# Rotary embedding from pairs of projected tiles, and layer 1's stack rows in another order

## What is computed

```python
# layer 1, on q and on k: head of 8 dimensions, halves t1 (0..3) and t2 (4..7)
t1, t2 = (t[..., :half], t[..., half:])
return jnp.concatenate([t1 * cos - t2 * sin, t1 * sin + t2 * cos], axis=-1)
...
# layer 2, on the 32 rotated dimensions of q: neighbours x0, x1
xr = xh.reshape(xh.shape[:-1] + (d // 2, 2))
x0, x1 = (xr[..., 0], xr[..., 1])
rot = jnp.stack([x0 * cos - x1 * sin, x0 * sin + x1 * cos], axis=-1)
...
x = x + _layernorm(_attn1(_layernorm(x)))      # layer 1
x = x + _layernorm(_layer2(_layernorm(x)))     # layer 2: attention, then the experts
```

## Time and profile before

| | |
|---|---|
| runs of the kernel before, us | 1727.74, 655.25, 657.92 (median 657.92) |
| the profiled execution, us | 656.71 |
| span of its trace, us | 655.0 |
| mean clock granted to PE | 0.947 of full |
| busy: PE, DVE, ACT, POOL, us | 564.1, 401.0, 310.4, 212.5 |
| DMA packets, data | 26657, 46.55 MB |

### The profile page before, as it was taken

The page is one execution under the profiler, slowest core; times in us unless marked ns, Lnnn a source line. Parts: engine busy times, 40 slices in busy tenths (PEclk is TensorE's granted clock), DMA queues, the critical chain, the costliest instruction groups (busy, mean ns, idle before and its releaser), DMA issues.

```text
span 655.0 us, 10075 instructions
## 1 busy us (share of the span) xinstructions
PE 564.1 (86%) x3634; PEld 311.1 (48%) x3634; DVE 401.0 (61%) x932; ACT 310.4 (47%) x589; POOL 212.5 (32%) x276
## 2 busy tenths in 40 slices
PE   3884998888887898999978999999999998899873
PEld 1732444444343454544435555545576446644642
DVE  6374877685684565675765675756646765534453
ACT  2311765666453664466434655554445432563221
POOL 4562444153442632660353211414322110220101
PEclk9685999999888899999998999999999999999987
DMA  9322113111334433211571122225314120000000
GB/s 269 103 88 102 39 46 111 59 53 41 122 111 77 114 88 128 110 67 61 103 182 46 56 51 42 47 77 116 92 21 86 30 51 1 19 2 1 0 18 16
DMA packets 26657, 46.55 MB, mean 71 GB/s; under 512 B 3216, under 2 KB 12336, under 8 KB 26032
## 3 DMA queue, kind: packets, MB, share of 16 engines
q1 hardware_dynamic: 26608, 45.91, 25.8%
HBM read 27.62 MB, written 17.83 MB: 69 GB/s over the span
## 4 chain that ended last, share of the span: by engine, by line
PE 60%; DVE 15%; SPq 6%; DMA 5%; ACT 5%; issue 4%; POOL 3%; DVEq 0%; POOLq 0%; ACTq 0%
PE ps L564 13%; PE ps L627 11%; PE ps L521 9%; PE ps L492 6%; DVE NM L1123 4%; PE ps L515 4%; PE ps L494 3%; PE ps L489 3%; PE ps L748 2%; DVE stats L1107 2%; PE ps L677 2%; SPq L441 2%; PE ps L571 2%; DMA KS<-scr_k 2%; PE ps L610 1%
## 5 line engine op out<-in xcount | busy, mean ns | idle before, releaser
L1123 DVE TENSOR_REDUCE NM<-ps 128x1 f32<-128x512 f32 (+3 forms) x352 | 219.3, 638 | 119.2 <-PE ps L494 111.5
L785 ACT ACTIVATE PG<-ps 128x512 f32<-128x512 f32 x320 | 181.5, 596 | 169.3 <-PE ps L521 86.8
L521 PE MATMUL ps<-QS,K 128*128 128x512 f32 x320 | 117.9, 453 | 0.0
L494 PE MATMUL ps<-maskb,identb 128*128 128x128 bf16 x512 | 108.8, 231 | 0.0
L564 PE MATMUL ps<-PG,V 128*32 128x512 f32 (+3 forms) x1024 | 97.9, 456 | 8.8 <-POOL PG L1070 6.2
L492 PE MATMUL ps<-K,QS 96*128 96x256 f32 (+3 forms) x256 | 83.6, 371 | 10.4 <-DVE NM L1123 10.2
L489 PE MATMUL ps<-KS,QS 96*128 96x256 bf16 (+3 forms) x256 | 72.3, 317 | 16.7 <-DVE NM L1123 15.6
L515 PE MATMUL ps<-QS,KS 128*128 128x128 bf16 (+3 forms) x256 | 64.1, 313 | 12.2 <-DMA QS<-MP 6.7
L1029 POOL TENSOR_TENSOR whole<-terms 128x512 f32<-128x512 f32 x28 | 35.5, 1269 | 109.4 <-DVEq L1216 107.8
L521 PEld LDWEIGHTS ps<-QS,K 128*128 128x128 f32 x320 | 50.9, 191 | 39.1 <-issue 19.6
L494 PEld LDWEIGHTS ps<-maskb,identb 128*128 128x128 bf16 x512 | 51.4, 100 | 38.0 <-issue 30.5
(11 more groups left out here) (153 smaller groups left out, 670.5 us busy)
## 6 DMA issues: line engine op xcount, KB each, us to landing
scr<-QC SPq DMA_DIRECT2D x24, 512.0 KB, 3.1
QS<-scr SPq DMA_DIRECT2D x32, 256.0 KB
QS<-scr_q SPq DMA_DIRECT2D x16, 288.0 KB
KS<-scr_k SPq DMA_DIRECT2D x16, 288.0 KB
QS<-scr SPq DMA_DIRECT2D x64, 64.0 KB
...
```

The lines of the kernel that those rows point to most:

```text
L494: return pe.matmul(dst[:, P * (k - 1):P * k], identb[:], maskb[:, 0, :], start=False, stop=True)
L521: mm = pe.matmul(bank.rearrange("p (h q) -> p h q", h=HG), keys[:, SEQ[n] % 2, P * j:P * j + P], QS2[:, heads, P * i:P * i + P], start=(ke ...
L785: act.activation(PG[:, n % 2, unit_place(LAYER[n], (u + k) % UNITS), :], ps[:, ST0 + (u + k) % 3, :], ACT.Exp, scale=scale).then_inc(exp_d ...
L1123: dve.tensor_reduce(dst, src, AX.X, ALU.max, negate=True).then_inc(fill_read, 1)
```

## The change

Three things are changed together.

1. **No turned projections.** In layer 1, `q1` projects two tiles whose rows are mixed: tile u holds the first halves of q (rows 0 to 63) and the second halves of k (rows 64 to 127), tile u + 1 the second halves of q and the first halves of k. `k1` has no projection any more. The new `rotation_of_pair` on DVE makes of the two tiles first u x cos and (u + 1) x sin, which POOL adds, then (u + 1) x cos and u x sin, which POOL subtracts. In layer 2, `ropeA` with part 0 (or 2) projects the even dimensions of two head groups into one tile and the odd ones into the next, by a view of the weights that takes every second column; parts 1 and 3 have no projection. Both tiles stay in their banks until the second job has read them.
2. **Slots.** `k1` goes into the slot of `q1`; `ropeA` 1 goes into the slot of `ropeA` 0, and `ropeA` 3 into that of `ropeA` 2. `ropeB` stays where it was.
3. **DRAM side.** Half tiles of 64 rows are stored (`store1`: 16 DMAs of 64 KB instead of 8 of 128 KB), layer 2's rotated rows are loaded by two DMAs of 16 rows for each part instead of one of 32 (`load2`: 8 DMAs for a head group instead of 6), and it waits for both tiles of the pair. In `load1` the 72 stack rows are ordered with the 24 (part, dimension) rows outside and the three copies inside; before, the three copies were outside. The weights are loaded without the turned halves, for layer 1 in four DMAs instead of one, three of them with runs of 64 numbers.

```diff
-        names = ("ln1", "ln1n", "x1T", "q1", "k1", "parts1", "parts1b", "store1")
-        return [(*slot, name, b, 0) for slot, name in zip((*at, at[-1]), names)]
+        return [(*slot, name, b, 0) for slot, name in zip((*at[:4], at[3], *at[5:], at[-1]), names)]
...
-                ((12, 3), "qabs", 1), ((12, 3), "kst2", 0), ((13, 0), "ropeA", 0), ((13, 1), "ropeB", 0),
-                ((13, 1), "ropeA", 1), ((13, 2), "ropeB", 1), ((13, 2), "ropeA", 2), ((13, 3), "ropeB", 2),
-                ((13, 3), "ropeA", 3), ((14, 0), "ropeB", 3), ((16, 3), "load2", 0), ((17, 0), "load2", 1),
+                ((12, 3), "qabs", 1), ((12, 3), "kst2", 0), ((13, 0), "ropeA", 0), ((13, 0), "ropeA", 1), ((13, 1), "ropeB", 0), ((13, 2), "ropeB", 1),
+                ((13, 2), "ropeA", 2), ((13, 2), "ropeA", 3), ((13, 3), "ropeB", 2), ((14, 0), "ropeB", 3), ((16, 3), "load2", 0), ((17, 0), "load2", 1),
...
-        QKV_LOADS = ((wqkv_sb[:], wqkv[:]), (rope1_sb[:], rope1[:]))
+        QKV_LOADS = ((wqkv_sb[:, 0:2, 0:64], wqkv[:, 0].rearrange("c (a m) -> c a m", a=2)),
+                     (wqkv_sb[:, 0, 64:P], wqkv[:, 2, 64:P]), (wqkv_sb[:, 1, 64:P], wqkv[:, 2, 0:64]),
+                     (wqkv_sb[:, 2], wqkv[:, 4]), (rope1_sb[:], rope1[:]))
...
-                    sp.dma_start(scr_q[b, a], qp[:, a, :]).then_inc(stored1, 16)
-                    sp.dma_start(scr_k[b, a], kp[:, a, :]).then_inc(stored1, 16)
-                    if a < 2:
-                        sp.dma_start(scr_k[b, 3 + a], kp[:, a, :]).then_inc(stored1, 16)
+                    sp.dma_start(scr_q[b, a, 0:64], up[0:64, a, :]).then_inc(stored1, 16)
+                    sp.dma_start(scr_q[b, a, 64:P], vp[0:64, a, :]).then_inc(stored1, 16)
+                    for copy in ((a, 3 + a) if a < 2 else (a,)):
+                        sp.dma_start(scr_k[b, copy, 0:64], vp[64:P, a, :]).then_inc(stored1, 16)
+                        sp.dma_start(scr_k[b, copy, 64:P], up[64:P, a, :]).then_inc(stored1, 16)
...
-                sp.dma_start(QS1[0:72, heads, :], bass.AP(q_parts.tensor, q_parts.offset, [[0, 3], *q_parts.ap]))\
-                  .then_inc(stack1_in[g], 16)
-                sp.dma_start(KS1[0:72, heads, :], bass.AP(k_parts.tensor, k_parts.offset, [[P * T, 3], *k_parts.ap]))\
-                  .then_inc(stack1_in[g], 16)
+                rows = [[H * T, 24], [0, 3], [1, HG * T]]
+                sp.dma_start(QS1[0:72, heads, :], bass.AP(scr_q, (3 * b * P + HG * g) * T, rows)).then_inc(stack1_in[g], 16)
+                rows = [[H * T, 24], [P * T, 3], [1, HG * T]]
+                sp.dma_start(KS1[0:72, heads, :], bass.AP(scr_k, (5 * b * P + HG * g) * T, rows)).then_inc(stack1_in[g], 16)
...
-                    sp.dma_start(QS2[DK2 * a + LAT:DK2 * a + DK2, heads, :].bitcast(F32),
-                                 scr_2[b, 2 + g, a].rearrange("(h d) t -> d h t", h=HG)).then_inc(stack2_in[g], 16)
+                    for odd in range(2):
+                        rows = scr_2[b, 2 + pair + odd, a, 64 * (g % 2):64 * (g % 2) + 64]
+                        sp.dma_start(QS2[DK2 * a + LAT + odd:DK2 * a + DK2:2, heads, :].bitcast(F32),
+                                     rows.rearrange("(h i) t -> i h t", h=HG)).then_inc(stack2_in[g], 16)
...
             def ropeA(b, part):
+                if part % 2:
+                    return
                 pe.wait_ge(xT2_ready, b + 1)
+                w = wqr_sb[:, part:part + 2, :].rearrange("c g (h i two) -> c (g h) i two", i=ROPE // 2, two=2)
                 for k in range(2):
-                    project(BANK0["ropeA", b, part] + k, wqr_sb[:, k, part, :], xT2[:])
+                    project(BANK0["ropeA", b, part] + k, w[:, :, :, k], xT2[:])
...
+            def rotation_of_pair(u, j, second, table):
+
+                if j >= 2:
+                    dve.wait_ge(job_done[j % 2], j // 2)
+                for k in range(2):
+                    bank = u + (1 - k if second else k)
+                    last = dve.tensor_tensor(terms[:, j % 2, k, :], full(bank), table[:, k, :], ALU.mult)
+                    if second:
+                        last.then_inc(bank_read[bank_of(bank)], 1)
+                if second:
+                    dve.wait_ge(*was_read(u))
+                    dve.sem_inc(terms_ready, 1)
+                else:
+                    last.then_inc(terms_ready, 1)
```

More of the change, by code:

```diff
@@ L108, in beside @@
                 ((7, 1), "x2T", 0), ((7, 2), "kst", 0), ((7, 2), "latv", 0), ((7, 3), "qabs", 0), ((7, 3), "kst2", 0),
-                ((8, 0), "qabs", 1), ((8, 0), "ropeA", 0), ((8, 1), "ropeB", 0), ((8, 1), "ropeA", 1),
-                ((8, 2), "ropeB", 1), ((8, 2), "ropeA", 2), ((8, 3), "ropeB", 2), ((8, 3), "ropeA", 3),
-                ((9, 0), "ropeB", 3), ((9, 1), "load2", 0), ((9, 3), "load2", 1), ((10, 2), "load2", 2),
+                ((8, 0), "qabs", 1), ((8, 0), "ropeA", 0), ((8, 0), "ropeA", 1), ((8, 1), "ropeB", 0), ((8, 2), "ropeB", 1),
+                ((8, 2), "ropeA", 2), ((8, 2), "ropeA", 3), ((8, 3), "ropeB", 2), ((9, 0), "ropeB", 3), ((9, 1), "load2", 0), ((9, 3), "load2", 1), ((10, 2), "load2", 2),
                 ((11, 2), "load2", 3))
@@ L168 @@
         TURN_OF.append(_n[0])
-    _n = [a + t for a, t in zip(_n, TAKES.get(_stage, (0, 0, 0, 0)))]
+    _takes = "ropeA2" if _stage == "ropeA" and _part % 2 else _stage
+    _n = [a + t for a, t in zip(_n, TAKES.get(_takes, (0, 0, 0, 0)))]
 BANK = []
@@ L453, in load2 @@
             def load2(b, g):
-                tiles = [QTILE["qabs", b, 0], QTILE["qabs", b, 1], QTILE["ropeB", b, g]]
+                pair = 2 * (g // 2)
+                tiles = [QTILE["qabs", b, 0], QTILE["qabs", b, 1], QTILE["ropeB", b, pair], QTILE["ropeB", b, pair + 1]]
                 for k in range(2):
@@ L634, in q1 @@
                     project(BANK0["q1", b, 0] + k, wqkv_sb[:, k, :], xT1)
-            def k1(b, _):
-                for k in range(2):
-                    project(BANK0["k1", b, 0] + k, wqkv_sb[:, 2 + k, :], xT1)
             def v1(b, _):
@@ L765, in _ @@
             stream(main, dict(
-                y3part=y3part, turnmax=turnmax, x1T=turn_tile("x1T"), q1=q1, k1=k1, v1=v1, wprod=wprod, wturn=wturn, o1T=o1T,
+                y3part=y3part, turnmax=turnmax, x1T=turn_tile("x1T"), q1=q1, v1=v1, wprod=wprod, wturn=wturn, o1T=o1T,
                 o1y=outputs("o1y", lambda b: ONT_AFTER["o1T", b], [wo1_sb[:]]), x2T=turn_tile("x2T"), kst=kst, latv=latv,
@@ L819, in parts1 @@
             def parts1(b, _):
-                for k, (stage, parts) in enumerate((("q1", qp), ("k1", kp))):
+                for k, (stage, parts) in enumerate((("q1", up), ("k1", vp))):
                     j = JOB0[stage, b, 0]
@@ L1028, in _ @@
                     pool.wait_ge(terms_ready, j + 1)
-                    pool.tensor_tensor(whole[:, j % 2, :], terms[:, j % 2, 0, :], terms[:, j % 2, 1, :], ALU.add)\
+                    pool.tensor_tensor(whole[:, j % 2, :], terms[:, j % 2, 0, :], terms[:, j % 2, 1, :], ops[part % 2])\
                         .then_inc(whole_ready, 1)
@@ L1089, in _ @@
             stream(main, dict(
-                clear2=clear2, ln1=scale("ln1", 0), q1=add_terms("q1"), k1=add_terms("k1"), parts1=parts1, parts1b=parts1b, v1c=v1c,
-                o1y2=scale("o1y2", 1), lna=lna, lna2=lna2, kst=add_terms("kst"), ropeA=add_terms("ropeA"), ropeB=ropeB,
+                clear2=clear2, ln1=scale("ln1", 0), q1=join_terms("q1", [ALU.add]), k1=join_terms("k1", [ALU.subtract]), parts1=parts1, parts1b=parts1b, v1c=v1c,
+                o1y2=scale("o1y2", 1), lna=lna, lna2=lna2, kst=join_terms("kst", [ALU.add]),
+                ropeA=join_terms("ropeA", [ALU.subtract, ALU.add]), ropeB=ropeB,
                 o2y=scale("o2y", 2), y3=scale("y3", 3), fin=fin))
@@ L1217, in rotation, with q1, k1, ropeA @@
                 return _
+            def rotation_of_pair(u, j, second, table):
[11 more added lines that the diff above has]
+                    last.then_inc(terms_ready, 1)
+            def q1(b, _):
+                if b == 0:
+                    dve.wait_ge(loaded_qkv, ALL_QKV)
+                rotation_of_pair(BANK0["q1", b, 0], JOB0["q1", b, 0], False, rope1_sb)
+            def k1(b, _):
+                rotation_of_pair(BANK0["q1", b, 0], JOB0["k1", b, 0], True, rope1_sb)
+            def ropeA(b, part):
+                rotation_of_pair(BANK0["ropeA", b, part - part % 2], JOB0["ropeA", b, part], part % 2 == 1, ropeq_sb)
             def wprod(b, _):
```

50 lines of the change are left out of this document (22 added, 28 removed), and 1 row of the table TAKES.

## The result

The changed kernel takes 651.11 us (median of 11 runs, 643.89 to 654.12) against 657.92: the ratio is 0.9887, with a 95% interval of 0.9863 to 0.9911, a gain of 7.4 us. Forecast were 643 us and a gain of 13.1, with 636 to 648 by the bounds of the terms. The profiled execution took 647.78 us, its span is 646.1.

The account below looks back on a forecast made before the run. PE was taken as the bound, with DVE close behind. From the profiled 656.7 us, 6.7 + 0.9 + 6.2 - 0.7 = 13.1 came off, giving 643.6, stated as 643; 636 to 648 by the terms' bounds, range 631 to 653.

Parts of the forecast that it names:

- Part 1: Layer 1's stack loads at the start: the new row order uses more DMA engines, and PE's 6.7 us stall goes.
- The later 0.9 us: PE's wait for a later load of layer 1's stack: claimed to go, 0.9 us gained.
- Part 3: More and smaller DMAs: `store1`'s extra issues hidden at the start, `load2`'s two more cost 0.7 us, weight loads nothing.
- Part 2, the start: `k1`'s removed projections in batches 0 and 1: 1.1 us gained (0 to 2.7).
- Layer 1's pair: `k1`'s removed projections: gains of 1.1 us at the start, 0.5 and 0.7 us in batches 2 and 3.
- Part 2, batch 1: Layer 2's `ropeA` in batch 1: removed products offset by `o1T`'s longer wait for a bank, 0 us (-2 to 2).
- Part 2, the rest: Layer 2's `ropeA` in the other batches: gains of 1.4 us in batch 0, 0.5 in batch 2, 2.0 in batch 3.
- A: Rival: PE is the bound everywhere, ten removed pairs of products count in full, 17.9 us; 630.8 us, chance 0.12.
- B: Rival: loads stay narrow, the stall and the 0.9 us stay, DVE waits 3.2 us for a store; 654.4 us, chance 0.09.
- D: Rival: slower, DVE stands behind late stores in layer 2's rotation, 20.7 us of waits; 668.2 us, chance 0.07.
- D's sign of 3 us: What would show the slower rival: DVE's multiplications waiting for `job_done` for over 3 us.
- C: Rival: DVE's lateness and held banks eat the ten pairs' whole saving; 648.7 us, up to 653, chance 0.12.

Follow-up runs that it names:

- the kernel with all edits and layer 1's pair: The changed kernel with batch 0's `v1` in PSUM bank 5, batch 2's `o1T` ahead of batch 1's first `ropeA`, and 12 store issues per batch: 643.04 us, ratio 0.9768.
- Wide loads alone: The kernel before with only the order of layer 1's stack rows in `load1` changed, 24 rows outside the three copies: 652.38 us, ratio 0.9914.
- B's kernel: The changed kernel with the old order of the stack rows in `load1`, three copies outside: 669.06 us, ratio 1.0174.

## Why the forecast was half right

The direction and the largest term were right, but the gain is 5.7 us short of the forecast and 651 us lies above its 648. The steps that failed are named in 2 to 4.

1. *Part 1* held: the order of rows took the 6.7 us stall away (-6.8 in the table), with 12 engines and 192 GB/s, inside the 147 to 254 assumed. The first score wasn't at 55 us but at 58.5; 2.8 us of it is the start, which came 1.7 us later and not 1.1 earlier. "The later 0.9 us goes too ... even if its issue is later by part 3" failed: the wait is 1.6 us. With full stores it does go.
2. *Part 3 is the step that failed most, by the runs.* "Store1 has 8 more, 3.6 us for a batch", hidden at the start. It was priced by the issue of a full store, and only the start was asked for its cover. It is 6.2 us of SP, covered at the start, and uncovered at batch 1's stack: 2.5 us where 0 was summed. The four more DMAs for weights and tables were checked against the table that DVE wants, not against the last table that `wprod` waits for, which was issued 2.1 us later.
3. *Part 2, the start*, forecast -1.1, came out +1.7. The forecast took PE's products at the speed of before. But the clock fell at 19 to 20 us where it had held to 22, `wprod` took 1.7 us longer, and batch 1's two products took 3.78 us, not 2.7. `v1`'s wait of 1.98 us for the pair's bank, which the forecast never named though it did so for `o1T`, stands ahead of that fall, but made `v1` only 0.35 us later itself; that it brings the fall about is not shown: in the kernel with all edits and layer 1's pair `v1` has no such wait, and the clock is down all the same from 20 us on (0.60 between 20 and 21). Wide loads alone, without any pair, also had +1.1 at the start, by the clock as well. Layer 1's pair was put at 2.3 us in all and is worth about 0.
4. *Part 2, batch 1*: 0 (-2 to 2) came out +3.9. The wait was foreseen at the right size (3.25 us), the low clock behind it was not: the sum let 1.8 us of removed products pay for 2.0 us of waiting, and by the short stretches above the clock alone cost 1.6. Moving one entry brought 3.3 us back.
5. *Part 2, the rest* held: layer 2's pairs with wide loads gave 4.4 us more than wide loads alone (10.1 - 5.7), against 3.2 forecast with `load2`'s part, which was put at 0.7 and shows as 0.1 in PE's wait (4.2 us for 4.1). Batches 0 and 2 gave more, batch 3 less. POOL's wait in batch 2 is still there, as forecast, with 1.95 us for 3.03, and ACT's wait of 3.23 us in batch 1 has gone, as forecast.
6. *Rivals.* A is refuted by the waits behind DVE. B's kernel was measured, and it was not 654 but 669: what B named is there (ACT waits 3.12 us for the store), but batch 1's narrow load behind 16 half stores, which holds PE for 6.5 us where B left 0.9, and a start 3.9 us late were in no rival. D's wait exists, DVE for POOL's split, but with 4.5 us in all and 1.35 at most in layer 2's pairs it is far from the 20.7 that D summed; one wait behind POOL passed D's sign of 3 us, 3.29 us ahead of `kst` in batch 3, in a stretch that still came out 1.6 us faster. C is close in number, for another reason: layer 2's pairs did save time, as 5 says.
7. *Slips in the working*, too small to explain the miss: by its own rows the fourth multiplication at the start would end 1.3 us earlier, not 0.6 (5.36 + 0.69 against 2.68 + 3 x 0.69), and 177.8 + 1.4 is 179.2, not 179.4.

In sum, from 13.1: wide loads by themselves 1.9 less than forecast, half stores 2.5, layer 1's pair 2.3, layer 2's 1.2 more; 13.1 - 1.9 - 2.5 - 2.3 + 1.2 = 7.6, against 7.4. Each of these terms is a difference of two ratios whose intervals are 3 to 6 us wide, so that they close is partly luck. How much of the 1.9 is PE's clock stays open: no run held the clock at one level, and runs of the same changed program lie from 643.9 us at a mean clock of 0.960 to 653.4 at 0.931.
